# Expert blocks of 128, 160 or 224 rows with a body for each size, where there were blocks of 128 or 160

## The reference, cut to what matters

```python
x = x + _L0_xattn_ref(_layernorm(x), ctx_768, ctx_768, ...)
...
# mixture of experts: B*S = 512 rows, D = 512, E = 8 experts, H = 2048, top_k = 2
logits = jnp.einsum('bsd,de->bse', x, router_w) + router_b
top_vals, top_idx = jax.lax.top_k(logits, top_k)
keep = jax.nn.one_hot(top_idx, E, dtype=logits.dtype).sum(-2) > 0
gating = jax.nn.softmax(jnp.where(keep, logits, NEG_INF), axis=-1)
h = jax.nn.relu(jnp.einsum('td,edh->eth', xf, w1) + b1[:, None, :])
y = jnp.einsum('eth,ehd->etd', h, w2) + b2[:, None, :]
out = jnp.einsum('etd,te->td', y, gf)
```

## Time and profile before

| | |
|---|---|
| median of 3 runs | 1129.09 us (1127.59 to 1132.04) |
| the profiled execution's own time | 1132.11 us |
| its span in the trace | 1130.4 us |
| the loop over blocks, to its last `sum_outputs` | 797 to 1116.3 us |
| after it | 14.1 us |
| PE, DVE, ACT, POOL busy | 95, 88, 65, 45% of the span |
| granted TensorE clock, mean | 0.987 of 2.4 GHz |
| read from HBM | 130.88 MB |

### The profile page before, as it was taken

The page is one execution under the profiler, slowest core; times in us unless marked ns, Lnnn a source line. Parts: engine busy times, 40 slices in busy tenths (PEclk is TensorE's granted clock), DMA queues, the critical chain, the costliest instruction groups (busy, mean ns, idle before and its releaser), DMA issues.

```text
span 1130.4 us, 24025 instructions
## 1 busy us (share of the span) xinstructions
PE 1079.5 (95%) x7583; PEld 1029.9 (91%) x7584; DVE 993.2 (88%) x2266; ACT 732.6 (65%) x1515; POOL 504.1 (45%) x447
## 2 busy tenths in 40 slices
PE   5999999999999999999999999998889999899996
PEld 4899999999999999999999999987778998789885
DVE  7579989989989989899999998988889888998995
ACT  3756565656666666666565656664668777787774
POOL 5565656566647565656575565361112021220211
PEclk9999999999999999999999999999889999999998
DMA  5322121222121112122212211044888877888783
GB/s 193 105 76 68 43 81 42 66 59 63 45 78 47 63 51 71 52 62 57 62 42 80 60 48 50 4 159 150 243 250 255 278 242 231 263 269 275 247 262 106
DMA packets 86369, 138.48 MB, mean 123 GB/s; under 512 B 15817, under 2 KB 40521, under 8 KB 86337
## 3 DMA queue, kind: packets, MB, share of 16 engines
q1 hardware_dynamic: 82800, 130.07, 36.2%
q0 software_dynamic: 3536, 8.00, 3.5%
HBM read 130.88 MB, written 7.17 MB: 122 GB/s over the span
## 4 chain that ended last, share of the span: by engine, by line
PE 75%; DVE 11%; issue 5%; ACT 5%; DMA 2%; DVEq 1%; POOL 0%; SPq 0%; ACTq 0%; POOLq 0%
PE ps L433 13%; PE ps L435 13%; PE ps L434 13%; PE ps L1498 8%; PE ps L1654 8%; PE ps L1548 8%; PE ps L1529 4%; PE ps L1530 4%; PE ps L1655 3%; DVE h_mix L1336 2%; DVE w_lo L1218 2%; DVE h_sum L1330 1%; DVE w_lo L1226 1%; DMA w_raw<-in_w_dram 1%; ACT w_hi L870 1%
## 5 line engine op out<-in xcount | busy, mean ns | idle before, releaser
L587 POOL TENSOR_TENSOR ctx_hi<-ctx_raw,no_query 128x1152 fp32r<-128x1152 f32 x64 | 142.0, 2219 | 262.8 <-PE ps L435 251.8
L820 ACT ACTIVATE probs<-ps,negmax 128x1152 f32<-128x1152 f32 x64 | 78.4, 1225 | 185.0 <-DVE negmax L1149 185.0
L1050 DVE SCALAR_TENSOR_TENSOR k_mix<-ps,bk_sb,k_mix 64x384 fp32r<-64x384 f32 (+1 forms) x256 | 162.3, 634 | 37.8 <-ACT k_mix L773 32.8
L433 PE MATMUL ps<-wv_hi,ctx_hi 128*128 128x256 f32 (+1 forms) x624 | 180.7, 290 | 2.3 <-DVE k_mix L1050 2.1
L591 POOL TENSOR_TENSOR ctx_lo<-ctx_raw,ctx_hi 128x1152 fp32r<-128x1152 f32 x64 | 179.8, 2809 | 5.0
L435 PE MATMUL ps<-wv_hi,ctx_lo 128*128 128x256 f32 (+1 forms) x624 | 175.0, 280 | 0.0
L434 PE MATMUL ps<-wv_lo,ctx_hi 128*128 128x256 f32 (+1 forms) x624 | 174.6, 280 | 0.0
L1654 PE MATMUL ps<-xg_mix,w_hi 128*128 128x320 f32 (+1 forms) x584 | 158.5, 344 | 13.6 <-DVE h_sum L1330 11.8
L773 ACT ACTIVATE k_mix<-ps,bk_sb 64x384 fp32r<-64x384 f32 (+1 forms) x256 | 151.0, 590 | 22.8 <-PE ps L435 18.3
L1655 PE MATMUL ps<-xg_mix,w_lo 128*128 128x160 f32 (+1 forms) x584 | 135.7, 232 | 0.0
L1654 PEld LDWEIGHTS ps<-xg_mix,w_hi 128*128 128x128 f32 x584 | 112.8, 193 | 22.5 <-DVE h_sum L1330 17.0
(11 more groups left out here) (235 smaller groups left out, 2628.4 us busy)
## 6 DMA issues: line engine op xcount, KB each, us to landing
w_raw<-in_w_dram SPq DMA_DIRECT2D x76, 1024.0 KB, 5.9
ctx_raw<-in_ctx_t_dram SPq DMA_DIRECT2D x48, 576.0 KB, 3.8
ctx_raw<-in_ctx_t_dram SPq DMA_DIRECT2D x16, 673.5 KB, 4.1
out_dram<-acc POOLq DMA_DIRECT2D x2, 1024.0 KB, 11.6
q_both<-q_scratch SPq DMA_DIRECT2D x14, 128.0 KB, 3.0
x<-in_x_dram SPq DMA_DIRECT2D x4, 256.0 KB, 3.4
wq_raw<-in_wq_dram SPq DMA_DIRECT2D x1, 1024.0 KB, 8.1
q_scratch<-q_out SPq DMA_DIRECT2D x1, 1024.0 KB, 7.4
```

Source lines behind the costliest of these rows:

```text
L433: pe.matmul(acc_ap, a_hi, b_hi, start=start, stop=False)
L587: nc.gpsimd.tensor_tensor(ctx_hi[slot][:, :, 0:n], ctx_raw[slot][:, :, 0:n], no_query[:].rearrange("p (o i) -> p o i", o=1).broadcast_to([ ...
L1050: last = nc.vector.scalar_tensor_tensor(out=k_mix[other, 2 * a + i, cols], in0=ps[rows, bank, 0:m], scalar=bk_sb[rows, a:a + 1], in1=k_mix ...
```

## The change

BLOCK becomes 224 (REST = 96), WIDE = 160 keeps the old size, and a block has one of three sizes. The table cuts every 224 rows; `kind` replaces `narrow` and is 0 for up to 128 rows, 1 for up to 160, 2 above. With the counts above there are eight blocks: 97, 74, 148, 154, 127, 62, 214 and 148 rows, of kinds 0, 0, 1, 1, 0, 0, 2, 1.

PE and DVE get a body for each size, behind nested Ifs on `kind`. ACT keeps one body and does 160 columns of each step; in a block of 224 DVE does columns 160 to 223 of the bias (`rest_parted`) and of the relu's high part (`rest_high`) as well. In a block of kind 0 DVE now works on 128 columns and leaves `sum_outputs` out. DVE's steps 0 and 1 are in the body, so its jump and its loads of registers now stand between `sum_outputs` and step 0. PE's `hidden(b + 1, 0)`, `turn_outputs` and `hidden(b + 1, 1)` stand behind the bodies, in two copies (160 and 224 rows) behind an If on the next block's kind, with an If on this block's kind inside. `turn_rows` does first the four transposes of 128 rows, then the four of the rest. The selection, the gather and the split of the gathered rows have 224 rows for every block. `yt` moves to another place in SBUF and its columns from 160 on are cleared once.

```diff
-    REST = P // 4
+    REST = 3 * P // 4
     BLOCK = P + REST
+    WIDE = P + P // 4
...
             def low_term(b, c):
...
-                nc.scalar.activation(h_part[:, c % 2, :], ps[:, hidden_bank(c), BLOCK:2 * BLOCK], ACT.Identity,
+                nc.scalar.activation(h_part[:, c % 2, 0:WIDE], ps[:, hidden_bank(c), BLOCK:BLOCK + WIDE], ACT.Identity,
...
-            def sum_hidden(b, c):
+            def sum_hidden(b, c, n):
 
                 dve.wait_ge(h_parted, HT * b + c + 1)
-                nc.vector.tensor_tensor(h_sum[:, c % 4, :], ps[:, hidden_bank(c), 0:BLOCK], h_part[:, c % 2, :],
+                if n > WIDE:
+                    nc.vector.tensor_scalar(h_part[:, c % 2, WIDE:n], ps[:, hidden_bank(c), BLOCK + WIDE:BLOCK + n],
+                                            b1_cur[:, 0, c:c + 1], None, ALU.add).then_inc(rest_parted, 1)
+                    dve.wait_ge(rest_parted, HT * b + c + 1)
+                nc.vector.tensor_tensor(h_sum[:, c % 4, 0:n], ps[:, hidden_bank(c), 0:n], h_part[:, c % 2, 0:n],
                                         ALU.add).then_inc(h_summed, 1)
...
+            def relu_high_rest(b, c, n):
+
+                if n > WIDE:
+                    dve.wait_ge(h_summed, HIDDEN_AHEAD + HT * b + c + 1)
+                    nc.vector.tensor_scalar(h_mix[:, c % 4, 0, WIDE:n], h_sum[:, c % 4, WIDE:n], 0.0, None,
+                                            ALU.max).then_inc(rest_high, 1)
+
+            def relu_low(b, c, n):
+
+                if n > WIDE:
+                    dve.wait_ge(rest_high, HT * b + c + 1)
                 dve.wait_ge(h_high, HT * b + c + 1)
...
-            nc.vector.tensor_scalar(narrow[:], left2[:], float(P), None, ALU.is_le).then_inc(narrow_ready, 1)
+            step(nc.vector.tensor_scalar(left[:], left2[:], float(P), None, ALU.is_gt))
+            step(nc.vector.scalar_tensor_tensor(out=start[:], in0=left2[:], scalar=float(WIDE), in1=left[:],
+                                                op0=ALU.is_gt, op1=ALU.add))
+            nc.vector.tensor_copy(kind[:], start[:]).then_inc(kind_ready, 1)
             take_bias(slice(0, 1))
             gathered_low(0)
-            sum_hidden(0, 0)
-            w2_low_piece(0, 0)
-            relu_low(0, 0)
-            sum_hidden(0, 1)
-            w2_low_piece(0, 1)
-            relu_low(0, 1)
+            for piece in range(PIECES):
+                w2_low_piece(0, piece)
             take_rows(0)
...
+            def block_low(b, expert_next, n):
+
+                if n <= WIDE:
+                    dve.sem_inc(rest_parted, HT)
+                    dve.sem_inc(rest_high, HT)
+                for c in range(HT):
+                    sum_hidden(b, c, n)
+                    relu_high_rest(b, c, n)
...
                 take_bias(bass.ds(expert_next, 1))
-                sum_outputs(b)
-                for c in range(HIDDEN_AHEAD):
-                    sum_hidden(b + 1, c)
-                    weight_low(b + 1, c)
-                    relu_low(b + 1, c)
+                if n > P:
+                    sum_outputs(b, n)
+                else:
+                    dve.sem_inc(y_summed, KD)
+
+            dve.wait_ge(kind_ready, 1)
+            with dve.Fori(0, blocks) as b:
+                expert_next = dve.value_load(table[0:1, bass.ds(b + 1, 1)], min_val=0, max_val=E - 1)
+                size = dve.value_load(kind[0:1, bass.ds(b, 1)], min_val=0, max_val=2)
+                with dve.If(size < 1):
+                    block_low(b, expert_next, P)
+                with dve.Else():
+                    with dve.If(size < 2):
+                        block_low(b, expert_next, WIDE)
+                    with dve.Else():
+                        block_low(b, expert_next, BLOCK)
...
             def turn_rows(b, moved):
...
-                for half in range(2):
-                    for k in range(2):
-                        for u in range(BT):
-                            n, d = ROWS[u], slice((2 * half + k) * P, (2 * half + k + 1) * P)
+                for u in range(BT):
+                    n = ROWS[u]
+                    for half in range(2):
+                        for k in range(2):
+                            d = slice((2 * half + k) * P, (2 * half + k + 1) * P)
...
             with pe.Fori(0, blocks) as b:
-                is_narrow = pe.value_load(narrow[0:1, bass.ds(b, 1)], min_val=0, max_val=1)
-                with pe.If(is_narrow > 0):
+                size = pe.value_load(kind[0:1, bass.ds(b, 1)], min_val=0, max_val=2)
+                size_next = pe.value_load(kind[0:1, bass.ds(b + 1, 1)], min_val=0, max_val=2)
+                with pe.If(size < 1):
                     block(b, P)
                 with pe.Else():
-                    block(b, BLOCK)
+                    with pe.If(size < 2):
+                        block(b, WIDE)
+                    with pe.Else():
+                        block(b, BLOCK)
+                with pe.If(size_next < 2):
+                    hidden(b + 1, 0, WIDE)
+                    finish(b, size)
+                    hidden(b + 1, 1, WIDE)
+                with pe.Else():
+                    hidden(b + 1, 0, BLOCK)
+                    finish(b, size)
+                    hidden(b + 1, 1, BLOCK)
```

More of the change, by code:

```diff
@@ L83, in bass_perceiver_layer_kernel @@
     TOP_K = 2
-    REST = P // 4
+    REST = 3 * P // 4
     BLOCK = P + REST
+    WIDE = P + P // 4
+    SIZES = (P, WIDE, BLOCK)
     ROWS = (P, REST)
@@ L88, in bass_perceiver_layer_kernel @@
     MOST = -(-T // BLOCK)
+    assert 2 * BLOCK <= 480
     assert TT == D // P
@@ L221, in bass_perceiver_layer_kernel @@
         xg_mix = place("xg_mix", [P, KD, 2, BLOCK], F32R, moe)
-        yt = place("yt", [P, KD, BLOCK], F32, moe)
         pad_to(LOW, "moe_pad", moe)
@@ L236, in bass_perceiver_layer_kernel @@
         gates_mix = place("gates_mix", [LANES, T], F32R, moe)
-        place("stage2_rest", [P, 3 * KD - BT - 1, D], F32, moe)
+        place("stage2_mid", [P, 2 * KD - BT - 1, D], F32, moe)
+        yt = place("yt", [P, KD, BLOCK], F32, moe)
+        place("stage2_rest", [P, KD * (D - BLOCK)], F32, moe)
         rw_raw = place("rw_raw", [P, KD, E], F32, moe)
@@ L289, in bass_perceiver_layer_kernel @@
         left2 = sb("left2", [P, TABLE], F32, moe)
-        narrow = sb("narrow", [P, TABLE], I32, moe)
+        kind = sb("kind", [P, TABLE], I32, moe)
         table_f = sb("table_f", [P, TABLE + 1], F32, moe)
@@ L695, in _ @@
             nc.gpsimd.memset(idx_next[:].bitcast(F32), 0.0).then_inc(rows_cleared, 1)
+            nc.gpsimd.memset(h_sum[:, :, P:WIDE], 0.0).then_inc(rows_cleared, 1)
             pool.wait_ge(numbers_ready, 6)
@@ L926, in relu_high @@
                 act.wait_ge(h_summed, HIDDEN_AHEAD + HT * b + c + 1)
-                nc.scalar.activation(h_mix[:, c % 4, 0, :], h_sum[:, c % 4, :], ACT.Relu).then_inc(h_high, 1)
+                nc.scalar.activation(h_mix[:, c % 4, 0, 0:WIDE], h_sum[:, c % 4, 0:WIDE], ACT.Relu).then_inc(h_high, 1)
             def weight_high(b, c):
@@ L1406, in _ @@
             blocks = dve.value_load(table[0:1, TABLE:TABLE + 1], min_val=1, max_val=MAX_BLOCKS)
-            for piece in range(PIECES):
-                w1_low_piece(1, piece)
-            with dve.Fori(0, blocks) as b:
-                expert_next = dve.value_load(table[0:1, bass.ds(b + 1, 1)], min_val=0, max_val=E - 1)
-                for c in range(HIDDEN_AHEAD, HT):
-                    sum_hidden(b, c)
+            def block_low(b, expert_next, n):
[5 more added lines that the diff above has]
+                    relu_high_rest(b, c, n)
                     if c == HT - 1:
-                        relu_low(b, c)
+                        relu_low(b, c, n)
                         gathered_low(b + 1)
@@ L1426, in _ @@
                 take_bias(bass.ds(expert_next, 1))
-                sum_outputs(b)
-                for c in range(HIDDEN_AHEAD):
-                    sum_hidden(b + 1, c)
-                    weight_low(b + 1, c)
-                    relu_low(b + 1, c)
+                if n > P:
[13 more added lines that the diff above has]
+                        block_low(b, expert_next, BLOCK)
+            for c in range(HIDDEN_AHEAD):
+                sum_hidden(blocks, c, WIDE)
         @block.tensor
```

35 lines of the change are left out of this document (18 added, 17 removed).

## The result

The change makes the kernel slower: 1154.95 us in the median of 5 runs (1152.36 to 1157.07) against 1129.09, a ratio of 1.022 with a 95% interval of 1.020 to 1.025. 1109.6 was forecast, with 1120 as the upper end. The profiled execution took 1152.36 us, with a span of 1150.6.

A forecast was written before the change was run, and what follows sets the result against it. It took PE to bound wide blocks and DVE narrow ones; -70.6 + 45.5 + 0.9 - 1.6 + 3.0 + 3.0 + 0.3 = -19.5 us, from the median 1129.1 to 1109.6 us, range 1102 to 1120.

The forecast's parts named there:

- first jumps over code that was never run: Block ends on PE and DVE: PE's known stall stays, DVE gets one first jump too; +3 us (0 to 6).
- rival 1: Code is fetched again at every block, 6 us a block, +42 at seven further block ends: 1152 us; chance 0.09.
- The sign that was named for it: Profile after: jumps over 1 us at each block, not at the end of block 0 alone, would mean rival 1 holds.
- pair of 448 and 224 columns on PE: Two matmuls in the block of 214 rows: 0.315 us a pair, bounds 0.28 and 0.36.
- DVE's step in the block of 214: DVE's five operations of one step sum to 2.28 us, against PE's 2.52 us.
- eight transposes of gathered rows, to the next matmul's start: `turn_rows` on PE, grouped by shape, should come to 1.1 us, -0.6 us a wide block.
- blocks 6 and 7 become one: Their 70.6 us go and a block of 214 rows at 45.5 us (43 to 51) comes: gain 25.1 us.
- wide blocks, three: Grouped transposes gain 0.6 us, DVE's later jumps and loads cost 0.8, larger selection 0.1: +0.3 each, +0.9 in all.
- narrow blocks 1, 4, 5: Blocks where DVE is the bound: fewer columns, no reductions, but exposed jumps and loads; -0.4 us each.
- block 0: The first block: -0.4 us as a narrow block, +3.0 (1 to 6) for DVE's later step 2.
- sum over the loop: The forecast's terms for all blocks and first jumps: -19.8 us; the full sum, with +0.3 at the end, was -19.5.
- The trace's argument on code: Attention loops of 1427 instructions on PE and 296 on DVE jump back without a stall; the new ones have 1656 and 378.

The follow-up runs named there:

- experiment 1: The changed kernel with only two bodies on DVE, 160 and 224 (narrow blocks use 160), a loop of 273 instructions, PE unchanged: 1115.91 us, ratio 0.988.
- experiment 8: experiment 1 with an untaken branch over 102 memsets at the head of DVE's loop, making it 378 instructions: 1149.24 us.
- experiment 11: experiment 1 with a branch inside DVE's 160 body that leaves out the reductions for blocks of up to 128 rows: 1115.50 us.
- experiments 3 to 7: The kernel before, with untaken branches in DVE's loop over 128, 192, 224, 256 or twice 128 memsets: 1130.9, 1133.0, 1209.9, 1208.3, 1213.2 us.
- 1208.3 us run: The kernel before with one untaken branch over 256 memsets in DVE's loop, making it 371 instructions: 1208.3 us.
- 192 memsets: The kernel before with one untaken branch over 192 memsets in DVE's loop, making it 307 instructions: 1133.0 us.
- experiment 10: experiment 1 with PE's bodies in the order 224, 160, 128: 1115.08 us.
- experiment 9: The kernel before with only the order of the transposes in `turn_rows` as changed, grouped by their number of rows: 1127.14 us, ratio 0.998.

## Why the prediction was wrong, point by point

The step that failed is "first jumps over code that was never run": it gave DVE's code a price once, 3 us with 6 as the upper bound, and held that the loop is there afterwards. In its place DVE's loop of 378 instructions was fetched again in every pass: DVE stood seven times, 56 us in all, and 33 of the 39 us between the kernel changed and experiment 1 come back with the loop's length alone (experiment 8). That is rival 1, which had a chance of 0.09, in part: it is DVE's loop alone that is fetched again, and by its length, not by how far a jump goes. That its 1152 us lie near the measured 1155 is in good part luck: its 6 us a block were read from a long jump on PE, while DVE's stands, of 3.7 to 12.6 us, cost 5.6 a block (39 us over seven), and the forecast that it was added to was itself some 6 us too low (1115.91 for 1109.6). The sign that was named for it, a jump of over 1 us at each block, would have missed it: DVE's jumps at L1455 and L1458 are recorded with at most 69 ns, and the stand shows only as idle time with no releaser and as packets on q14. For each term, what experiment 1 shows of it, where DVE's loop is held:

| step | forecast | measured |
|---|---|---|
| pair of 448 and 224 columns on PE | 0.315 us | 0.315 |
| DVE's step in the block of 214 | 2.28 us | 2.28 |
| eight transposes of gathered rows, to the next matmul's start | 1.1 us | 0.71 |
| blocks 6 and 7 become one | -70.6 + 45.5 | -70.6 + 43.09 |
| wide blocks, three | +0.9 | +0.5 (block 2), +5.0 (block 3), +2.5 (the last) |
| narrow blocks 1, 4, 5 | -0.4 each | +1.5, +0.8, +0.6 |
| block 0 | -0.4 + 3.0 | +1.5 |
| first jumps | +3.0 | in the blocks above |
| sum over the loop | -19.8 | -15.2 |

The first three are read in the block of 214 of the kernel changed, between its stands; two pairs on PE from 1067.38 to 1068.01, DVE from `h_sum` to `h_sum`, and the transposes from 1089.64 to 1090.35 (the recorded duration of the eight is 0.93):

```profile
1067.38 0.38 PE L1691 MATMUL ps<-h_mix,w_hi 128*128 128x448 f32 x1
1067.60 0.27 PE L1692 MATMUL ps<-h_mix,w_lo 128*128 128x224 f32 x1
1067.70 0.38 PE L1691 MATMUL ps<-h_mix,w_hi 128*128 128x448 f32 x1
...
1068.01 0.38 PE L1691 MATMUL ps<-h_mix,w_hi 128*128 128x448 f32 x1
```

```profile
1066.18 0.39 DVE L1341 TENSOR_TENSOR h_sum<-ps,h_part 128x224 f32<-128x224 f32 x1
1066.61 0.20 DVE L1348 TENSOR_SCALAR h_mix<-h_sum 128x64 fp32r<-128x64 f32 x1
1066.71 1.22 DVE L1225 TENSOR_TENSOR w_lo<-w_raw,w_hi 128x1024 fp32r<-128x1024 f32 x1
1067.85 0.38 DVE L1356 SCALAR_TENSOR_TENSOR h_mix<-h_sum,h_mix 128x224 fp32r<-128x224 f32 x1
1068.15 0.28 DVE L1338 TENSOR_SCALAR h_part<-ps,b_cur 128x64 f32<-128x64 f32 x1
1068.46 0.39 DVE L1341 TENSOR_TENSOR h_sum<-ps,h_part 128x224 f32<-128x224 f32 x1
```

- *Two blocks become one*: right, the gain was 27.5 us for 25.1 in experiment 1; in the kernel changed the stand leaves 15.4 of it. PE and DVE are near each other, as the sum had it (40.99 and 41.10 us busy in 43.09).
- *Wide blocks*: the jumps and loads at the block's end, with code held, are nearly hidden: in experiment 1 `h_sum` of step 0 follows the reductions at once at the end of blocks 4 and 6 (984.43 and 1.67, then 986.02; 1061.71 and 2.21, then 1063.91), and with 0.26 us of "issue" at the end of block 3. The last block's +2.5 has 1.0 that was overlooked: a wide block stands behind another one now, as block 3 of before did (37.04). Block 3's +5.0 is PE's second long jump, at the end of block 2, 5.1 us in experiment 1 (5.7 in the kernel changed). The prediction had one such jump on PE, which was there before, and put the first jump over the body of 224 rows, for a block of 160, at nothing: of its own terms this is the largest error that is left once DVE's loop is held.
- *Narrow blocks*: experiment 1 runs them with 160 columns on DVE and keeps the reductions, so the forecast of -0.4 isn't tested by it alone. Without the reductions (experiment 11), but still with 160 columns, blocks 4 and 5 are 0.1 shorter and 0.3 longer than before: near nothing.
- *Block 0*: step 2 of DVE comes 11.5 us behind the bias (803.52 for 792.00) where it was 8.8 (801.73 for 792.97), +2.8 for +3.0. The block as a whole grew by 1.5 only.
- *The trace's argument on code*: that an attention loop of 296 instructions on DVE is held was the last size the trace could show, and it said nothing of 378. The bound was drawn from it all the same. A bound for what the trace does not show should have been the price of a fetch at each pass.

Outside the loop little moved: the kernel changed takes its first bias 2.7 us earlier (790.25 for 792.97) and has a tail of 14.03 us for the earlier trace rows's 14.11. -2.7, +23.0 in the blocks and -0.1 are the 20.2 us by which the span grew. The 2.7 says nothing of the change: in the kernels of experiments 3 to 7, whose work up to there is that of before, the first bias comes at 790.4 to 793.7.

## What to carry to other kernels

A loop with several bodies is a choice on the size of each engine's code, engine by engine. Count the instructions between a loop's head and its jump back in the built program, branches not taken included, and compare with the largest loop that a trace shows without fetches in later passes; past that, reckon with a price for each pass and not one for the kernel. Where a body can be left out on the engine that holds the shorter loop and kept on the one where it pays, do that: here DVE with two bodies and PE with three is 1.2% faster than before, and no version measured beats it by more than the measurement can tell, where three on both are 2.2% slower.

## What the runs showed of the hardware

- VectorE's loop of 307 instructions is held, one of 339 is fetched again in every pass (q14: 15 packets against 55; 36.34 us for block 2 against 46.77). The Trainium skill (Runtime: NRT & Kernel Launch, Instruction fetch mechanics) gives most engines 512 instructions, TensorE 2048; these runs do not bear out the 512 as the length of a loop that VectorE holds. Where in between the limit lies, and whether it depends on where the loop starts, was not tried.
- The price of a pass in block 2: 10.7 us where the stand falls behind step 1 (1208.3 us run, 47.04 for 36.35 with 192 memsets), 5.8 where it falls behind the reductions (experiment 8, 42.31 for 36.55). Why the two differ by so much is open.
- TensorE's loop of 1656 instructions is held: in the kernel changed nothing arrives on q8 after 922.5 us. But a first jump over a body that was never run costs 3.3 us to 5.7, and the two of experiment 10 6.5 and 7.7. The last three packets of q8 start at 916.8, 916.9 and 922.5 us, in and just behind the jump of 915.3 to 921.0, and none comes when the body jumped over first runs; it looks as if that jump waited for the code that it skips. This was not tested, nor whether an early pass through the code would hide it.
- Idle time on PE is paid twice: around the stands its clock was granted at 1.2 GHz, and block 2 of the kernel changed has PEclk 0.89 for 1.00 in experiment 1, with 35.13 us busy for 33.83.
- Eight transposes on TensorE whose shapes take turns (128 and 32 rows) have a pitch of 1.67 us together, the same eight grouped by shape 0.89 (experiment 9).
